# Layer 0's mixing as plain fp32 products in the four quarters of TensorE's array

## What is computed

```python
# layer 0, mixing: x is (128, 64, 1024)
att = softmax(h @ W2 + b2)                                  # (128, 8), h from two gelu layers of cond
agg_w = einsum('bk,koi->boi', att, weight[..., 0])          # one 64 x 64 matrix for each sample
y = einsum('boi,bih->boh', agg_w, x) + (att @ bias_k)[:, :, None]
# layer 0, dense part
base = einsum('bsd,od->bso', y, W_base) + b_base            # 1024 x 1024
...                                                         # gates, low rank products A and B
x = x + base + moe
# layer 1: a grouped convolution over 9 taps, and a dense part of the same kind
```

## Time and profile before

| | us |
|---|---|
| median of 3 runs (lowest to highest) | 2148.48 (2147.06 to 2154.15) |
| the profiled execution, its own time | 2151.52 |
| the profiled execution, its span | 2149.9 |
| TensorE busy with matmuls | 2136.5 (99% of the span) |
| VectorE busy | 1613.7 (75%) |
| GpSimd busy | 1014.2 (47%) |
| ScalarE busy | 509.6 (24%) |

### The profile page before, as it was taken

The page is one execution under the profiler, slowest core; times in us unless marked ns, Lnnn a source line. Parts: engine busy times, 40 slices in busy tenths (PEclk is TensorE's granted clock), DMA queues, the critical chain, the costliest instruction groups (busy, mean ns, idle before and its releaser), DMA issues.

```text
span 2149.9 us, 43337 instructions
## 1 busy us (share of the span) xinstructions
PE 2136.5 (99%) x12663; PEld 2097.0 (98%) x12663; DVE 1613.7 (75%) x5379; ACT 509.6 (24%) x1180; POOL 1014.2 (47%) x1311
## 2 busy tenths in 40 slices
PE   8999999999999999999999999999999999999999
PEld 8999999999999999999999999999999999999998
DVE  5878888888788788788776766776776776776776
ACT  4222222222222222222322222222222222222221
POOL 5675655656656656656633333333333333333332
PEclk9999999999999999999999999999999999999999
DMA  5443343343343343333543333343333344333342
GB/s 212 129 111 103 91 111 102 98 107 99 102 110 93 106 107 91 109 105 91 169 145 123 121 123 128 129 136 127 121 121 130 123 136 133 121 121 125 125 133 97
DMA packets 163309, 256.09 MB, mean 119 GB/s; under 512 B 21200, under 2 KB 103248, under 8 KB 163280
## 3 DMA queue, kind: packets, MB, share of 16 engines
q1 hardware_dynamic: 162944, 255.42, 38.8%
q10 hardware_dynamic: 336, 0.30, 0.1%
HBM read 121.62 MB, written 100.73 MB: 103 GB/s over the span
## 4 chain that ended last, share of the span: by engine, by line
PE 97%; DVE 0%; issue 0%; DMA 0%; SPq 0%; ACT 0%; DVEq 0%
PE psB L1060 74%; PE psB L1086 8%; PE psT L1035 3%; PE psT L1041 3%; PE psT L1039 3%; PE psT L1040 3%; PE psT L1036 1%; PE psB L1157 1%; SPq L381 0%; DMA Xraw<-in_x 0%; DMA shifted<-mixbuf 0%; PE psT L1031 0%; PE psT L1032 0%; PE psT L1033 0%; SPq L371 0%
## 5 line engine op out<-in xcount | busy, mean ns | idle before, releaser
L1060 PE MATMUL psB<-Whi,Yhi 128*128 128x384 f32 x3024 | 716.5, 344 | 0.9 <-DVE outb L800 0.5
L1060 PE MATMUL psB<-Wlo,Yhi 128*128 128x384 f32 x3024 | 703.7, 340 | 0.0
L1060 PE MATMUL psB<-Whi,Ylo 128*128 128x384 f32 x3024 | 701.9, 339 | 0.0
L419 POOL TENSOR_TENSOR Xlo<-Xraw,Xhi 128x256 fp32r<-128x256 f32 x504 | 390.9, 806 | 463.3 <-ACT Xhi L543 463.3
L1060 PEld LDWEIGHTS psB<-Wlo,Yhi 128*128 128x128 f32 x3024 | 549.3, 189 | 0.1
L1060 PEld LDWEIGHTS psB<-Whi,Ylo 128*128 128x128 f32 x3024 | 549.1, 189 | 0.0
L1060 PEld LDWEIGHTS psB<-Whi,Yhi 128*128 128x128 f32 x3024 | 522.1, 189 | 13.8 <-issue 1.6
L916 DVE STREAM_TRANSPOSE HT<-hw 32x32 f32<-32x32 f32 x1968 | 397.6, 202 | 25.2
L440 POOL TENSOR_TENSOR res<-res,bias 128x256 f32<-128x256 f32 x256 | 183.3, 748 | 394.9 <-DMA res<-x_scratch 394.9
L800 DVE TENSOR_TENSOR outb<-psB,res 128x384 f32<-128x384 f32 (+1 forms) x384 | 225.6, 673 | 147.8 <-PE psB L1086 147.8
L559 ACT CAST Yhi<-Y 128x512 fp32r<-128x512 f32 x256 | 157.2, 622 | 565.1 <-DVE Y L748 283.4
(11 more groups left out here) (133 smaller groups left out, 2068.1 us busy)
## 6 DMA issues: line engine op xcount, KB each, us to landing
x_scratch<-outb SPq DMA_DIRECT2D x64, 512.0 KB, 2.7
x_block_scratch<-outb SPq DMA_DIRECT2D x512, 64.0 KB, 2.0
Xraw<-x_block_scratch SPq DMA_DIRECT2D x64, 512.0 KB, 4.8
res<-x_scratch SPq DMA_DIRECT2D x64, 512.0 KB, 4.4
out<-outb SPq DMA_DIRECT2D x64, 512.0 KB, 3.0
Xraw<-in_x SPq DMA_DIRECT2D x62, 512.0 KB, 3.4
shifted<-mixbuf SPq DMA_DIRECT2D x128, 224.0 KB, 2.5
row<-row_scratch SPq DMA_DIRECT2D x126, 64.0 KB, 4.2
```

The costliest lines, as they stand in the source:

```text
L419: last = pool.tensor_tensor(Xlo[:, piece], x_tile(j, par)[:, piece], as_f32(Xhi[:, piece]), ALU.subtract)
L1060: last = mm(psB[:, 3 * par + b, 0:cols], y, w[:, k, BANK0[b]:BANK0[b] + cols], start=(k == 0 and y is yh and w is Whi), stop=(k == KT - 1 ...
```

## The change

- Layer 0's mixing has no hi and lo any more: `x_tile` and `M`, both fp32, are multiplied as they are. `high_x`, `low_x` and `low_m` are gone from layer 0; `place_m` copies agg to M's diagonal. `M` is 128 x 128.
- Tiles 3 to 63 (`in_squares`) are mixed by `mix_squares`: each of the 8 blocks is four products of 64 x 64 operands with 64 columns, one for each quarter of the array (row half a: the sample; column half m: the half of the block), the two samples in two different banks of `psT`. All 32 stand together behind base's first block, and their waits (`ready_to_mix`) ahead of that block. Tiles 0, 1 and 2 are mixed by one plain 128 x 128 product for a block.
- DVE takes Y from `psT` by one addition for a chunk instead of two (L748 is gone).
- Step 1 on TensorE: two `Wlo` products of tile 0 first, mix of tile 2 after k = 2, 4, 5, 7 (`MIX_AFTER_SECOND`), the turn after k = 1 and `up` after k = 3. POOL's, ACT's and DVE's first steps are put in another order around that.
- SP's waits on `x_hi` and `x_lo` ahead of loading a tile of layer 0 go.
- The last `emit` takes the columns of the first bank ahead of the wait for the second.

```diff
+MIX_AFTER_SECOND = (2, 4, 5, 7)
...
-        M = sb("M", [P, 2, P], F32R)
+        M = sb("M", [P, P])
...
+        def in_squares(n, layer):
+
+            return layer == 0 and not (isinstance(n, int) and n < 3)
...
-            low_x(0, 0, 0)
-            low_x(0, 1, 0)
             split_lo(KT - 2, 0)
...
             pool.wait_ge(s_hi, 1)
-            low_up(0, range(0, 2))
+            low_up(0, range(PIECES))
+            split_lo(KT - 1, 0)
             pool.wait_ge(bias_in, 16)
             residual(0, 0, 0)
-            low_x(1, 0, 0)
-            split_lo(KT - 1, 0)
...
-            def high_m(n):
-                act.wait_ge(agg_ready, n + 1)
-                nc.scalar.copy(M[0:C, 0, 0:C], agg[0:C, :])
-                nc.scalar.copy(M[C:P, 0, C:P], agg[C:P, :]).then_inc(m_hi, 1)
+            def place_m(n):
+                act.wait_ge(agg_ready, n + 1)
                 if not (isinstance(n, int) and n == 0):
                     act.wait_ge(mixed, NC * n)
+                nc.scalar.copy(M[0:C, 0:C], agg[0:C, :])
+                nc.scalar.copy(M[C:P, C:P], agg[C:P, :]).then_inc(m_ready, 1)
...
-                        nc.vector.tensor_tensor(y, bank[:, :, 0, :], bcast(row[:, par, :], 1, 2), ALU.add).then_inc(y_part, 1)
-                        dve.wait_ge(y_part, NC * (n if isinstance(n, int) and n == 0 else n - SUMMED) + c + 1)
-                        nc.vector.tensor_tensor(y, bank[:, :, 1, :], y, ALU.add).then_inc(y_chunk, 1)
+                    if layer == 0:
+                        if in_squares(n, layer):
+                            a = c % 2
+                            bank = psT[:, a, h * CH:(h + 1) * CH].rearrange("p (k o) -> p k o", o=C)
+                            y = Y[:, h * HB:(h + 1) * HB].rearrange("p (k b o) -> p k b o", b=2, o=C)[:, :, a, :]
+                            add = bcast(row[:, par, a * C:(a + 1) * C], 1, KT // 2)
...
+                        nc.vector.tensor_tensor(y, bank, add, ALU.add).then_inc(y_chunk, 1)
...
+            def ready_to_mix(j, par):
+
+                n = 2 * j + par
+                wait_for_x(pe, j, par)
+                pe.wait_ge(m_ready, n + 1)
+                if not (isinstance(n, int) and n == 0):
+                    pe.wait_ge(y_chunk, NC * n)
+
+            def mix_squares(j, par):
+
+                half = slice(0, C), slice(C, P)
+                for k in range(KT):
+                    for m in range(2):
+                        for a in range(2):
+                            last = mm(psT[half[m], a, k * C:(k + 1) * C],
+                                      x_tile(j, par)[half[a], k * P + m * C:k * P + (m + 1) * C],
+                                      M[half[a], half[a]], start=True, stop=True)
+                last.then_inc(mixed, NC)
...
-                        mm(to, Xhi[:, xs], M[:, :, :].rearrange("p s n -> p (s n)"), start=True, stop=False)
-                        last = mm(to[:, 0:P], Xlo[:, xs], M[:, 0, :], start=False, stop=True)
+                    if layer == 0:
+                        last = mm(psT[:, c % 2, t * P:(t + 1) * P], x_tile(j, par)[:, xs], M[:, :], start=True, stop=True)
...
+                    for k in range(2):
+                        base_part(0, k, True)
                     for k in range(KT - 2):
                         base_part(1, k, False)
-                    for k in range(KT):
+                    for k in range(2, KT):
                         base_part(0, k, True)
-                        if k % 2 == 0:
-                            mix(1, 0, 0, k // 2)
...
+                squares = lay1 == 0 and in_squares(n + 1, 0)
+                if squares:
+                    ready_to_mix(*after(j, par))
                 for k in range(KT):
                     base(j, par, lay, k)
+                    if k == 0 and squares:
+                        mix_squares(*after(j, par))
```

More of the change, by code:

```diff
@@ L411, in split_lo, with low_x @@
                 last.then_inc(w_loP, 1)
-            def low_x(j, par, layer):
+            def low_x(j, par):
                 n = 2 * j + par
                 w = H // PIECES
-                pool.wait_ge(x_hi, n + 1)
+                pool.wait_ge(x_hi, n - STEPS + 1)
                 for i in range(PIECES):
                     piece = slice(i * w, (i + 1) * w)
-                    last = pool.tensor_tensor(Xlo[:, piece], x_tile(j, par)[:, piece], as_f32(Xhi[:, piece]), ALU.subtract)
+                    last = pool.tensor_tensor(Xlo[:, piece], Xraw[:, par, piece], as_f32(Xhi[:, piece]), ALU.subtract)
                 last.then_inc(x_lo, 1)
@@ L502, in step @@
                     split_y(*after(j, par), range(0, 1))
-                if lay2 is not None and not (isinstance(j, int) and n == 0):
-                    low_x(j + 1, par, lay2)
+                if lay2 == 1:
+                    low_x(j + 1, par)
                 if splits:
@@ L627, in step @@
                     split_y(*after(j, par), 0, range(0, 1))
-                    if lay2 is not None:
-                        high_x(j + 1, par, lay2)
+                    if lay2 == 1:
+                        high_x(j + 1, par)
                     if lay0 is not None:
@@ L792, in emit @@
                 to = outb[:, par, :].rearrange("p (r q) -> p r q" if layer == 0 else "p (q r) -> p r q", r=BR)
-                for b, (r0, r1) in enumerate(EIGHTHS):
-                    if very_last and b == 1:
-                        dve.wait_ge(up_done, n + 2)
-                    if b < 2:
-                        product = psB[:, 3 * par + b, 0:BANKN[b]].rearrange("p (r q) -> p r q", q=Q)
-                    else:
-                        product = psB[:, 3 * par:3 * par + 2, BANKN[0]:HB]
-                    last = nc.vector.tensor_tensor(
-                        to[:, r0:r1, :], product,
-                        res[:, par, :].rearrange("p (r q) -> p r q", r=BR)[:, r0:r1, :], ALU.add)
+                old = res[:, par, :].rearrange("p (r q) -> p r q", r=BR)
+                if very_last:
+                    for b in range(2):
+                        if b:
+                            dve.wait_ge(up_done, n + 2)
+                        whole, part = EIGHTHS[b], (EIGHTHS[2][0] + b, EIGHTHS[2][0] + b + 1)
+                        for (r0, r1), c0 in ((whole, 0), (part, BANKN[b])):
+                            product = psB[:, 3 * par + b, c0:c0 + (r1 - r0) * Q].rearrange("p (r q) -> p r q", q=Q)
+                            last = nc.vector.tensor_tensor(to[:, r0:r1, :], product, old[:, r0:r1, :], ALU.add)
+                else:
+                    for b, (r0, r1) in enumerate(EIGHTHS):
+                        if b < 2:
+                            product = psB[:, 3 * par + b, 0:BANKN[b]].rearrange("p (r q) -> p r q", q=Q)
+                        else:
+                            product = psB[:, 3 * par:3 * par + 2, BANKN[0]:HB]
+                        last = nc.vector.tensor_tensor(to[:, r0:r1, :], product, old[:, r0:r1, :], ALU.add)
                 last.then_inc(o_done, 1)
@@ L1029, in mix @@
                     xs = slice(k * P, (k + 1) * P)
-                    if layer == 0 and isinstance(n, int) and n in (1, 2):
-                        mm(to[:, 0:P], Xhi[:, xs], M[:, 0, :], start=True, stop=False)
-                        mm(to[:, 0:P], Xhi[:, xs], M[:, 1, :], start=False, stop=False)
-                        last = mm(to[:, 0:P], Xlo[:, xs], M[:, 0, :], start=False, stop=True)
-                    elif layer == 0:
-                        mm(to, Xhi[:, xs], M[:, :, :].rearrange("p s n -> p (s n)"), start=True, stop=False)
-                        last = mm(to[:, 0:P], Xlo[:, xs], M[:, 0, :], start=False, stop=True)
+                    if layer == 0:
+                        last = mm(psT[:, c % 2, t * P:(t + 1) * P], x_tile(j, par)[:, xs], M[:, :], start=True, stop=True)
                     else:
@@ L1213, in step @@
                     for c in range(NC):
-                        if k == mix_after[c] and lay1 is not None:
+                        if k == mix_after[c] and lay1 is not None and not squares:
                             mix(*after(j, par), lay1, c)
```

104 lines of the change are left out of this document (41 added, 63 removed).

## The result

The changed kernel takes **2109.4 us** (median of 4 runs, 2108.5 to 2111.9) beside 2148.3 us before (4 runs, 2147.1 to 2154.2): a ratio of 0.982, 95% interval 0.980 to 0.983. That is 38.9 us less, where 37.7 were forecast. The profiled execution took 2111.9 us, its span is 2110.1, 39.8 shorter than the span profiled before.

What follows compares the result with a forecast made beforehand. TensorE's issued work was taken to bound layer 0, with waits mattering at the start. Squares' 28.7 us plus the start's 9 gave 37.7 us less: 2111 us from the median, range 2102 to 2168.

Steps and rivals of the forecast that it cites:

- The bound: Layer 0 from 62 to 1030 us: time is the sum of what TensorE issues, busy 967.82 of 968.00 us.
- Squares, 0.93 us: A tile's 32 squares in layer 0: all four quarters run at once, 16 x 0.058 = 0.93 us.
- the bound of 0.072: Slower pace within a quarter, from L1101's matmuls: 16 x 0.072 = 1.15 us a tile, gaining 15 us over 61 tiles.
- Rival 1: Squares: row halves take turns or matmuls keep program order; block 2.26 us against 1.80, total 2167 us; chance 0.18.
- The round trip, 0.40 us: Leaving the whole array for quarters and coming back, once a tile: 0.40 us, possibly 0.30 for squares.
- Rival 2: Squares: TensorE is fed more slowly than four quarters work; at 0.02 a pair, block 1.68 us, total 2132; chance 0.20.
- Waits in layer 0: Waits ahead of block 0 and for `up`: cost 0, with 2.8 us of room for M and 1.0 for `up`.
- The start, 9 us: First steps, tiles 0 to 2: terms sum to 9.1, taken as 9 us gained, between 5 and 11.
- (e): Start: the slow clock stretch, 6.4 us at 0.52, would be 3.3 without the 2.80 gap: 3.1 us gained.
- the waits: Start: TensorE waits in pieces for DVE's `Wlo`, 1.8 us each to make; 1.2 us lost, too short for the clock to fall.
- no gap over 1 us: Sign at the start: TensorE shows no gap over 1 us after 30 us.
- tile 2's base at 51 to 52: Sign at the start: tile 2's base (L1060) begins at 51 to 52 us instead of 60.68.

Runs made afterwards that it cites:

- row halves alone: Changed kernel with 16 products a tile, x as 64 rows x 128 columns, only row halves side by side: 2162.1 us, beside 2111.2 for the changed kernel.
- runs of two: Changed kernel with the 32 squares ordered as two products of one quarter before the next quarter's turn: 2119.2 us.
- four undisturbed starts: Profiles with the clock at 1.00: changed kernel without squares, in two lots, twice as many, a quarter in a row; 2140.7, 2132.1, 2166.6, 2247.6 us.
- runs of four: Changed kernel with the 32 squares ordered as four products of one quarter before the next quarter's turn: 2204.1 us.
- runs of eight: Changed kernel with all 8 products of one quarter in a row, then all 8 of the next: 2247.6 us, ratio to before 1.047.

## Why the prediction was right

**The bound.** TensorE without a wait from 62 us on, before and after, and the time followed what it issues: in the six variants of the squares the change of the step times 61 is the change of the total within 2 us. The 367 us of work that VectorE and GpSimd lost gave nothing there: with all of it gone and no squares, the step is 0.05 us shorter.

**Squares, 0.93 us.** Shown twice: doubling them cost 0.934 a tile, and single starts are 58 ns apart in each quarter. The pace taken from L1101's loads was right, the bound of 0.072 not needed. The step that the rows of before could not carry, row halves at once, is shown by the row halves alone. Rival 1 (2167) would have needed 32 x 0.058.

**The round trip, 0.40 us.** It is 0.35; with 0.03 in what mixing cost before (1.28 + 0.547 is 1.83, not 1.80) the gain is 0.547 instead of 0.47 a tile, 33.4 instead of 28.7 us. This was the largest term that was mis-sized. The prediction had seen that L1168's value could be 0.30 for squares, and kept 0.40.

**Rival 2, feeding.** Its chance of 0.20 was for 64 pairs that can't be issued in 0.93 us. A matmul every 15 ns on average is kept up through 64 pairs, and 128. By the Trainium skill, "TensorE: Matmul & The Clock Gate", section "Wait — 56ns, not 53.3ns?", about 25 ns is the least between two starts. The trace disagrees for small products in different quarters: they start 6 to 7 ns apart.

**Program order.** By the Trainium skill, "TensorE: Matmul & The Clock Gate", Part 2, step 1, only weight loads are pulled ahead. The trace disagrees across quarters: products pass each other here (runs of two). But program order is not idle: with a quarter's products in one row the kernel lost 138 us to the changed one. The change's loop order, quarters innermost, is what the forecast's 0.93 rests on, and the prediction never said so; its rival 1 names the program's order in brackets, but prices it as two row halves taking turns (2167), where the wrong order costs 2248. That the changed kernel had the right loop order is luck as far as the forecast goes.

**Waits in layer 0.** None came, as costed. ACT (L544) has written M at 499.52 and block 0 starts at 503.91, 4.4 us of room:

```profile
499.28 0.24 ACT L544 COPY M<-agg 64x64 f32<-64x64 f32 x1
...
503.91 0.70 PE L1060 MATMUL psB<-Whi,Yhi 128*128 128x384 f32 x3
```

**The start, 9 us.** It gave 5.5 in the profiled execution. Two of its terms failed, (e) and the waits. The waits for `Wlo` are 2.7 us instead of 1.2: I had taken 1.8 us for one of VectorE's from rows in which GpSimd worked beside it, which was near (1.93), but let TensorE's own work cover more of it. The slow stretch (e) stayed in this execution for 3.4 us, 1.7 more than forecast. 9.1 - 1.5 - 1.7 = 5.9; the last 0.4 was not traced. The four undisturbed starts give 7.2 to 8.3. The forecast "no gap over 1 us" was wrong by 0.17, and "tile 2's base at 51 to 52" came true only when the residual was moved.

The two misses, +4.7 in the squares and -3.5 at the start, cancelled for the most part, and that is luck: the total is nearer than its terms.

## What to carry to other kernels

Small products in the four quarters of the array run side by side if they are written quarter by quarter in turn: 32 fp32 products of 64 x 64 take 0.93 us in turns, 1.09 in runs of two, 2.47 in runs of four and 3.18 in runs of eight. Put all of them in one lot, since each lot costs 0.35 us for the switch. Where VectorE's work is waited for, look at what GpSimd does in the same microseconds: here moving GpSimd's residual away gave 3.0 us, of which up to 1.7 may be the clock.

## What the runs showed of the hardware that I had not expected

- A product passes others in the program when its quarter is free; in three orders it got past at most three waiting matmuls (one and a half fp32 products) of a quarter. A quarter in use starts one each 58 ns (64 columns loaded, 64 streamed), and its second one 107 ns behind its first.
- On row halves, 128 columns loaded and 64 streamed go at 111 ns, as 128 and 128 on the whole array do.
- An fp32 addition or subtraction on GpSimd and a subtraction on VectorE of the same time slow each other: 7.9 against 3.9 us and 1.93 against 1.40 us.
- Gaps of at most 1.2 us at the start were followed by a fall of the clock to the lower level in five profiles and by none in four, all four from one chip; the old order's gap of 1.5 us was followed by none.
